# Attention's row maxima handed over by halves of a unit, four places for the split projection parts, and stack loads behind both transfers

## The reference

```
xn = layernorm(x)
xh = xn[:, :, :64];  xs = holt(xn)[:, :, :64]        # a smoothing scan over the tokens
s  = attention block: two multi-head attentions (8 heads of 8 numbers each), one over xh, one over xs,
     softmax(q k^T / sqrt(8)) v, output projections, layernorms, feed-forward
g  = silu(mixture of 32 experts, top 4 of 32 for each token, capacity 640 per expert, and a shared expert)
x  = x + s * g
```

## Time and profile before

| | |
|---|---|
| median of 3 runs | 2137.68 us (2133.76 to 2138.3) |
| profiled execution, its own time | 2140.73 us |
| its span, first to last instruction | 2138.9 us |
| PE busy | 1884.9 us (88%) |
| DVE busy | 1776.4 us (83%) |
| ACT busy | 1444.4 us (68%) |
| POOL busy | 344.0 us (16%) |
| mean granted TensorE clock | 0.936 |
| row maxima, first to last reduction | 139.8 to 1394.0 us |
| exponentials, first to last | 186.6 to 1444.2 us |

### The profile page before, as it was taken

How to read it: one execution, slowest core, us unless ns; L and a number is a source line. 1 busy time by engine, 2 the same in 40 slices (tenths; PEclk the granted TensorE clock), 3 DMA queues, 4 the chain that set the end, 5 groups by cost and what they waited for, 6 DMA issues and landing times.

```text
span 2138.9 us, 33478 instructions
## 1 busy us (share of the span) xinstructions
PE 1884.9 (88%) x11734; PEld 719.9 (34%) x11734; DVE 1776.4 (83%) x2689; ACT 1444.4 (68%) x2807; POOL 344.0 (16%) x516
## 2 busy tenths in 40 slices
PE   7537999999999999999999999988997887599884
PEld 6201222222222222222222222216764444266563
DVE  6689999999999999999999999903347887478778
ACT  5204888888888888888888888883322344567542
POOL 1210000000000222222222222000027652000000
PEclk9656999999999999999999999999998889799896
DMA  3231121120010111111111111016754332321321
GB/s 84 83 116 44 46 71 65 47 84 26 25 35 24 40 46 36 46 42 35 51 38 38 49 37 49 8 32 178 205 162 123 108 112 73 101 71 54 101 76 30
DMA packets 145888, 144.01 MB, mean 67 GB/s; under 512 B 29451, under 2 KB 124687, under 8 KB 145572
## 3 DMA queue, kind: packets, MB, share of 16 engines
q1 hardware_dynamic: 137380, 124.71, 19.2%
q0 software_dynamic: 8352, 17.29, 2.7%
HBM read 81.06 MB, written 60.03 MB: 66 GB/s over the span
## 4 chain that ended last, share of the span: by engine, by line
PE 70%; DVE 14%; ACT 8%; issue 3%; DMA 2%; SPq 2%; POOL 1%; DVEq 0%; ACTq 0%
PE PS L1606 23%; PE PS L1633 18%; PE PS L1588 8%; DVE mxp L758 6%; PE PS L1680 3%; ACT probs L1202 3%; ACT SG L1187 2%; PE PS L1736 2%; PE PS L1836 2%; PE PS L1854 1%; PE PS L1667 1%; PE PS L1745 1%; PE PS L1857 1%; PE PS L1839 1%; DMA xs_d<-SG 1%
## 5 line engine op out<-in xcount | busy, mean ns | idle before, releaser
L758 DVE TENSOR_REDUCE mxp<-PS 128x1 f32<-128x1024 f32 x1024 | 1203.5, 1220 | 43.9 <-PE PS L1588 29.2
L1202 ACT ACTIVATE probs<-PS 128x512 f32<-128x512 f32 x2048 | 1061.7, 604 | 168.1 <-PE PS L1633 164.9
L1633 PE MATMUL PS<-stacks 51*128 51x512 bf16 x2048 | 615.8, 383 | 28.2 <-ACT probs L1202 16.8
L1588 PE MATMUL PS<-stacks 48*128 48x512 bf16 x2048 | 518.9, 393 | 49.1 <-DVE mxp L758 30.4
L1606 PE MATMUL PS<-probs,VH 128*32 128x512 f32 x4096 | 546.7, 606 | 6.8 <-ACT SG L1187 6.1
L1633 PEld LDWEIGHTS PS<-stacks 51*128 51x128 bf16 x2048 | 154.3, 94 | 681.1 <-ACT probs L1202 611.7
L1588 PEld LDWEIGHTS PS<-stacks 48*128 48x128 bf16 x2048 | 109.5, 94 | 217.0 <-DVE mxp L758 178.0
L1472 POOL DMA_INDIRECT xe_d<-xn_s,rows_s x128 | 126.0, 984 | 328.5 <-PE PS L1606 292.6
L1497 POOL DMA_INDIRECT VP<-oe_d,ROWI x128 | 133.4, 1042 | 255.7 <-DMA oe_d<-stacks 194.7
L771 DVE TENSOR_TENSOR stacks<-stacks,PS 128x640 f32<-128x640 f32 x32 | 26.2, 820 | 134.7 <-ACT stacks L1234 134.7
L1606 PEld LDWEIGHTS PS<-probs,VH 128*32 128x32 f32 x4096 | 81.6, 108 | 125.0 <-issue 109.2
(11 more groups left out here) (344 smaller groups left out, 1922.4 us busy)
## 6 DMA issues: line engine op xcount, KB each, us to landing
xe_d<-zt SPq DMA_DIRECT2D x16, 640.0 KB
stacks<-xe_d SPq DMA_DIRECT2D x32, 320.0 KB, 3.3
oe_d<-stacks SPq DMA_DIRECT2D x32, 320.0 KB, 2.4
o_d<-SG SPq DMA_DIRECT2D x256, 32.0 KB, 1.6
ews<-in_ew_dram SPq DMA_DIRECT2D x33, 192.0 KB, 2.3
stacks<-ql_d SPq DMA_DIRECT2D x64, 96.0 KB
stacks<-kl_d SPq DMA_DIRECT2D x64, 96.0 KB
probs<-xs_d SPq DMA_DIRECT2D x18, 256.0 KB, 3.7
```

The source lines that it names most:

```text
L758: v.tensor_reduce(mxp[:, n // 2, n % 2:n % 2 + 1], MXB[n % 2].rearrange("p a c -> p (a c)"), X_AX, ALU.max).then_inc(mx_done, 1)
L1202: act.activation(probs[:, at:at + 512], PS[:, bank_of(u, e), :], ACT.Exp, scale=float(1.0 / np.sqrt(np.float32(DK)))).then_inc(exp_done, 1)
L1588: mm = pe.matmul(MXB[n % 2][:, i, :], QS[w][o:o + MAXROWS, (n // 2) * P:(n // 2 + 1) * P], KS[w][o:o + MAXROWS, key:key + 512], start=True ...
L1633: pe.matmul(PS[:, bank_of(u, e), :], KS[w][o:o + KROWS + 3, kt * P:(kt + 1) * P], QS[w][o:o + KROWS + 3, q0:q0 + 512], start=True, stop=Tr ...
```

## The change

Three edits, which depend on each other.

1. The split parts have four places; the two new ones lie in the stack slots 1 to 3, which are not loaded until all stores have landed. ScalarE's `lead(j)` waits for the stores of block j-4.
2. A unit's maxima are handed over in two halves, each of 8 query tiles (16 chunks, 1024 queries). Each half has its own reduction, GpSimd split, transposition, copy and pair of transfers. The unit's second half is turned after exponential 22 of the unit itself (TURNS = (22, 54)) and waited for at exponential 32; the next unit's first half after 54, as before. AHEAD falls from 10 to -6, so 26 chunks are made before the first exponential, and chunks run 16 fewer in front.
3. On SyncE the order for unit u is: clearing stores (first eight units), the second half's maxima of unit u, the loads for unit u+3 (into the slot of unit u-1), first output half, the first half's maxima of unit u+1, second output half.

```diff
-EXPS, TURN, AHEAD = 64, 54, 10
-SLOTS = EXPS + 1
+EXPS, TURNS, AHEAD = 64, (22, 54), -6
+SLOTS = EXPS + 2
...
         def part(parts, level, w):
-            return parts[level][:, w * 512:(w + 1) * 512]
+            if w < 2:
+                return parts[level][:, w * 512:(w + 1) * 512]
+            return QS[1 + level][:, ((parts is KPARTS) * 2 + w - 2) * 512:((parts is KPARTS) * 2 + w - 1) * 512]
...
-            def load_max(u, w):
-                hold(mt_out, u + 1)
+            def load_max(u, w, half, trip):
+                hold(mt_out, 2 * u + half + 1)
+                hold(m_ld[w], 64 * trip + 32 * half)
                 for o in (0, 64):
-                    sp.dma_start(QS[w][o + KROWS:o + KROWS + 3, :], mT[:, :]).then_inc(m_ld[w], 16)
+                    sp.dma_start(QS[w][o + KROWS:o + KROWS + 3, S // 2 * half:S // 2 * (half + 1)], mT[half][:, :]).then_inc(m_ld[w], 16)
...
+                    load_max(u, w, 1, k)
+                    if not last and w > 0 or w == 0 and not (isinstance(k, int) and k == 0):
+                        load_unit(u + 3, 2 * k + (w + 3) // 2, (w + 1) % 2, (w + 3) % 4)
                     store_half(u, g, w % 2, 0)
                     if not (last and w == 3):
-                        load_max(u + 1, (w + 1) % 4)
+                        load_max(u + 1, (w + 1) % 4, 0, k + (w == 3))
                     store_half(u, g, w % 2, 1)
...
-                    if not last:
-                        load_unit(u + 4, g + 2, w % 2, w)
...
-                v.wait_ge(mx_done, CHUNKS * (uu + 1))
-                after(v, spl_ready, uu)
-                v.tensor_reduce(nmx[:, 0, :], mxp[:, :, :], X_AX, ALU.max, negate=True).then_inc(nmx_ready, 1)
+                    if n % (CHUNKS // 2) == CHUNKS // 2 - 1:
+                        half = n // (CHUNKS // 2)
+                        tiles = slice(TCH // 2 * half, TCH // 2 * (half + 1))
+                        v.wait_ge(mx_done, CHUNKS * uu + n + 1)
+                        after(v, spl_ready, 2 * uu + half - 1)
+                        v.tensor_reduce(nmx[:, 0, tiles], mxp[:, tiles, :], X_AX, ALU.max, negate=True).then_inc(nmx_ready, 1)
...
-                after(act, ql_st, 48 * (j - 1))
-                after(act, kl_st, 48 * (j - 1))
+                after(act, ql_st, 48 * (j - 3))
+                after(act, kl_st, 48 * (j - 3))
...
-                    if e == TURN and not final:
-                        act.wait_ge(m_ld[w], 32 * (trip + 1))
-                        write_rows(u + 1, TURN_BANK[u])
+                    if e == TURNS[0]:
+                        after(act, m_ld[(u - 1) % 4], 64 * ((u - 1) // 4 + 1))
+                        write_rows(u, 1, TURN_BANK[u][0])
+                    if e == TURNS[1] and not final:
+                        act.wait_ge(m_ld[w], 64 * trip + 32)
+                        write_rows(u + 1, 0, TURN_BANK[u][1])
...
-                pe.wait_ge(m_ld[w], 32 * (u // 4 + 1))
                 for e in range(EXPS):
-                    after(pe, exp_done, EXPS * u + e - 2 + (TURN < e <= TURN + 2))
-                    if e == TURN + 3 and not final:
-                        pe.wait_ge(mt_out, u + 2)
+                    if e % (EXPS // 2) == 0:
+                        pe.wait_ge(m_ld[w], 64 * (u // 4) + 32 * (e // (EXPS // 2) + 1))
+                    after(pe, exp_done, EXPS * u + e - 2 + any(t < e <= t + 2 for t in TURNS))
+                    if e == TURNS[0] + 3:
+                        pe.wait_ge(mt_out, 2 * u + 2)
+                    if e == TURNS[1] + 3 and not final:
+                        pe.wait_ge(mt_out, 2 * u + 3)
```

More of the change, by code:

```diff
@@ L436, in _ @@
                     for lv in range(3):
[L437 removed]
+                        sp.dma_start(parts[lv, :, j * 512:(j + 1) * 512], part(src, lv, j % 4)).then_inc(stored, 16)
             hold(ql_st, 48 * NB)
@@ L676, in remainder @@
                 for n, (left, parts) in enumerate(((QREST, QPARTS), (KREST, KPARTS))):
-                    ins = v.scalar_tensor_tensor(left[w], PS[:, 4 + 2 * w + n, :], bcol[:, n:n + 1], part(parts, 0, w), ALU.add, ALU.subtract)
+                    ins = v.scalar_tensor_tensor(left[w], PS[:, 4 + 2 * w + n, :], bcol[:, n:n + 1], part(parts, 0, j % 4), ALU.add, ALU.subtract)
                 ins.then_inc(rest, 1)
@@ L1171, in middle @@
                 for left, parts in ((QREST, QPARTS), (KREST, KPARTS)):
-                    ins = act.activation(part(parts, 1, j % 2), left[j % 2], ACT.Copy)
+                    ins = act.activation(part(parts, 1, j % 4), left[j % 2], ACT.Copy)
                 ins.then_inc(part1, 1)
@@ L1431, in _ @@
                 for left, parts in ((QREST, QPARTS), (KREST, KPARTS)):
-                    ins = pool.tensor_tensor(part(parts, 2, j % 2), left[j % 2], part(parts, 1, j % 2), ALU.subtract)
+                    ins = pool.tensor_tensor(part(parts, 2, j % 4), left[j % 2], part(parts, 1, j % 4), ALU.subtract)
                 ins.then_inc(part2, 1)
@@ L1445, in _, with largest @@
             plink = Chain(pool, pool_chain).link
[L1447 to L1452, removed]
-                pool.tensor_tensor(spl[:, 2, :], nmx[:, 1, :], spl[:, 1, :], ALU.subtract).then_inc(spl_ready, 1)
+            def largest(uu, half):
+                tiles = slice(TCH // 2 * half, TCH // 2 * (half + 1))
+                first, second = nmx[:, 0, tiles], nmx[:, 1, tiles]
+                pool.wait_ge(nmx_ready, 2 * uu + half + 1)
+                after(pool, mt_ready, 2 * uu + half - 1)
+                plink(pool.tensor_copy(spl[:, half, 0, :], first))
+                plink(pool.tensor_tensor(second, first, spl[:, half, 0, :], ALU.subtract))
+                plink(pool.tensor_copy(spl[:, half, 1, :], second))
+                pool.tensor_tensor(spl[:, half, 2, :], second, spl[:, half, 1, :], ALU.subtract).then_inc(spl_ready, 1)
             def values(u):
@@ L1469, in scatter @@
                             pool.wait_ge(pv_done, TCH * (u - 3) + 2 * (KTOP * i + n))
-                        if i == 1 and n == 1:
-                            largest(u - 2)
+                        if n == 1:
+                            largest(u - 3 + i, 1 - i)
                         pool.indirect_dma_start(xe_d, bass.IndirectOffsetOnAxis(rows_s[i][:, n:n + 1], 0), xn_s[i][:, :], None,
                                                 bounds_check=E * CAP - 1, oob_is_err=False).then_inc(sc_st[i], 16)
-            for u in range(UNITS // 2):
+            for u in range(3):
                 values(u)
-                if u >= 2:
-                    largest(u - 2)
+            largest(0, 0)
+            for u in range(3, UNITS // 2):
+                values(u)
+                largest(u - 3, 1)
+                largest(u - 2, 0)
             pool.wait_ge(rows_done, 1)
@@ L1484, in _ @@
                 scatter(u)
-            for uu in range(UNITS - 2, UNITS):
-                largest(uu)
+            for uu in range(UNITS - 3, UNITS):
+                largest(uu, 1)
+                if uu + 1 < UNITS:
+                    largest(uu + 1, 0)
             for i in range(2):
@@ L1634, in _ @@
                               start=True, stop=True).then_inc(sc_ready, 1)
-                    if e == TURN and not final:
+                    if e == TURNS[0]:
                         pe.wait_ge(exp_done, EXPS * u + e - 1)
-                        turn_max(u + 1, TURN_BANK[u])
+                        turn_max(u, 1, TURN_BANK[u][0])
+                    if e == TURNS[1] and not final:
+                        pe.wait_ge(exp_done, EXPS * u + e - 1)
+                        turn_max(u + 1, 0, TURN_BANK[u][1])
                     if chunk < min(CHUNKS * UNITS, CHUNKS * (u + 1) + AHEAD + CHUNKS * (e + 1) // EXPS):
```

38 lines of the change are left out of this document (19 added, 19 removed).

## The result

The changed kernel takes 2111.67 us (median of 4 runs, 2110.06 to 2113.83), the kernel before beside it 2137.99 us: ratio 0.9877, 95% interval 0.9864 to 0.989. That is 26.3 us less where 19.3 were forecast; 2111.67 lies in the range and 6.7 us under the number.

The account below looks back on a forecast made before the run. Front waits, lone maxima, then 2048 exponentials at 0.6 us plus extras bound it, no engine full in the loop. -21.5 - 18.1 + 4.6 + 15.7 = -19.3 us: 2121.4 from the profiled run, 2118.4 from the median; range 2109 to 2130.

Parts of the forecast that it names:

- Four places: Front: ScalarE's waits for stores and VectorE's behind them vanish, maxima start at 118.3; -21.5 us, bounds 17.5 to 22.8.
- Fewer first chunks and the wait for the first transfer: Before the first exponential: 16 chunks fewer, -18.1 us; first scores wait behind the DMA backlog ending at 149.7, +4.6.
- no backlog in the way: Rival, first scores: the small transfer passes or the loads end sooner, 4.6 us less, 2113.8 us; chance 0.16.
- Halves in the loop: Loop: 32 more hand-overs at 0.49 us each, +15.7 us, bounds 10.9 to 28.8.
- 0.15 reduction: Loop: extra time of the four-exponential group with a unit's final reduction, 0.15 of the 0.49 us per hand-over.
- halving dearer: Rival, loop: a unit's second hand-over disturbs more, to 0.8 us a unit; +9.9 us, 2128.3; chance 0.14.
- The second wait for a transfer, and the loads behind both: Loop, exponential 32 and SP's queue: 2.3 us cover at the wait, 4.3 left after the loads; costed at nothing.
- The slower rival: Exponential 0 of each unit: stack loads not through at first half's hand-over; 2157 us if loads take 22; chance 0.06.
- What follows only moves: After attention: the rest of the span only shifts in time, its length unchanged; 0 us in the sum.

Follow-up runs that it names:

- e5: Changed kernel with the 2 MB store issued behind the first maxima's transfer; 2111.44 us, ratio 0.9875 to the kernel before.
- e3: Changed kernel without VectorE's wait for its own second small reduction at each unit's end; 2110.42 us, ratio 0.9873 to the kernel before.
- e7: Changed kernel with the stack loads back behind the second half's stores, for unit u+4 at the end of unit u; 2161.75 us, ratio 1.0119 to the kernel before.
- e1: Kernel before with only the four places for the split parts; 2120.62 us, ratio 0.9909 to the kernel before.
- e0: The kernel before, unedited, run and profiled again; 2137.59 us, ratio 0.9997 to the kernel before.
- e12: The changed kernel once more, unedited, beside e6 and e10 on one chip; 2195.84 us, ratio 0.9874 to the kernel before.
- e6: Changed kernel without VectorE's wait at each unit's end and with the 2 MB store behind the first maxima's transfer; 2192.13 us, ratio 0.9859 to the kernel before.
- e10: As e6, with two fewer chunks ahead of the first exponential (AHEAD = -8); 2191.1 us, ratio 0.9849 to the kernel before.

## Why the prediction was right, and where it was off

*Four places.* Right in kind: all six waits fell, and the ranks' matmuls then set L734. The term was 2.6 us too large: 18.9, not 21.5. The selection ends 3.2 us later than forecast, and L734 follows the ranks' matmuls 0.5 us sooner. Most of the 3.2 us can be added up from VectorE's rows: L718 (three times 1.53 for 0.69), L722 (three times 2.06 for 1.23) and L725 (1.53 for 0.69) are 5.9 us longer, and five of the six of L717 and L721 are 0.57 each shorter, 3.0 in all. Before, it was these that were long, beside GpSimd's remainders:

```profile
65.24 1.16 POOL L1432 TENSOR_TENSOR SG<-wa,HH 128x512 bf16<-128x512 f32 x1 [6.86 <-ACT wa L1172]
65.54 1.21 DVE L716 TENSOR_REDUCE EK<-probs 128x32 bf16<-128x1024 bf16 x1
...
66.78 1.80 DVE L717 TENSOR_TENSOR probs<-iob,EK 128x1024 bf16<-128x1024 bf16 x1
```

So the 5.6 us a block that I took over held one such clash a block, and without the waits other instructions meet the remainders, with a dearer clash. A remainder is longer too, 2.14 us for 1.16; the one that starts 0.1 us behind L717 or L721 is lengthened and they are not. A VectorE reduction with one input, L716 above, keeps its 1.21 beside a remainder. "SBUF — State Buffer" of the Trainium skill ("Who interferes with whom") has this as a rule: a VectorE instruction with two SBUF inputs contends with a GpSimd instruction that reads SBUF. The rows agree for L717 before and for L718 and L722 after; L725 has one tensor input and is outside this rule, and why it takes 1.53 was not tried. That the clashes are the cause is read off the overlap; no run took the remainders away.

*Fewer first chunks and the wait for the first transfer.* -13.2 against -13.5, and e5 and the packets showed the cause that I had named, the loads and behind them the store. That the size fits to 0.3 us is in part luck. The loads came 19.2 us earlier and not 22.8 (by the figures that the prediction gives, 20.2 and 1.2, it should have said 21.4), so the backlog ended 3.5 us after the forecast 149.7; the scores were needed 2.7 us after the forecast 146.3, because the front was late as well. The two errors nearly cancel. The rival "no backlog in the way" is refuted for the changed kernel.

*Halves in the loop.* +9.9 us against +15.7; this is the step that was mis-sized. "0.15 reduction" was read off the one group that held a reduction and also the wait at the unit's end. The rows after separate them, 2.40 against 2.53, and e3 removes 0.12 a unit by removing that wait. What is new is 0.33 for the transposition, and 32 times that is 10.6 us. The rival "halving dearer" has no row for it. The 2.7 us of slack that the prediction gave VectorE in a unit, for its lower bound, is 1.6 by the earlier trace rows ((1177.6 - 1130.0) / 30); the sum didn't use it.

*The second wait for a transfer, and the loads behind both.* Cost nothing in the changed kernel, as forecast: the wait before the first scores is the only one for L470's transfers in its list. The slower rival was the right thing to fear: with the loads ahead of the second half's transfer on the queue (e7) it cost 50 us.

*What follows only moves: not so.* In my sum the rest of the span was constant. It was 694.2 before and 687.3 after, and 685.7 to 693.0 over eight kernels timed at about 2110 to 2160 us whose code there is one and the same. Matching instruction by instruction, 1.4 us of the difference have come up 25 us behind the last weighing and 2.8 more between 165 and 195; at 566 it is still 4.1, and the rest comes up behind that, mostly between 570 and 590. Here the same two places of three kernels, 180 to 189 and 566 to 580 us behind the last weighing (the clock is the column behind GpSimd's). Before:

```profile
1624.70:1633.70 9.00, 7.61 (x18) 3.62 (x16) 6.43 (x33) 3.33 (x6) 6.41 (x7) 0.63 0.56 165
2010.70:2024.70 14.00, 7.41 (x17) 3.63 (x18) 9.41 (x29) 3.74 (x5) 0.00 (x0) 0.62 0.58 188
```

After:

```profile
1602.60:1611.60 9.00, 8.08 (x32) 4.22 (x33) 8.72 (x37) 2.94 (x6) 6.95 (x7) 1.00 0.60 168
1988.60:2002.60 14.00, 12.01 (x43) 6.43 (x42) 13.59 (x46) 8.75 (x12) 0.00 (x0) 0.92 0.71 230
```

e1, the four places alone:

```profile
1606.60:1615.60 9.00, 7.78 (x18) 3.69 (x17) 6.43 (x33) 3.15 (x5) 5.27 (x6) 0.64 0.57 160
1992.60:2006.60 14.00, 8.15 (x17) 3.92 (x18) 9.41 (x29) 3.74 (x5) 0.00 (x0) 0.50 0.58 188
```

Where TensorE has the clock at 1.00 or near it, it does 32 and 43 matmuls in the window; at 0.5 to 0.64 it does 18 and 17. Whether the higher clock makes the work faster there, or earlier work brings the clock up, the rows don't part, and what in the changed kernel shifts it is open. The seven kernels with the halves have 685.7 to 691.3, the three executions without them (before, e0, e1) 692.8 to 694.2, so it goes with the halves, by how much varies, and it isn't shown to be theirs. So of the 26.3 us, about 22 lie within attention, where the edits are, and the rest behind it, which no term of the sum held; without it the forecast would have been some 3 us off and not 6.7.

## What to carry to other kernels

A small transfer that the next step waits for must not be queued behind large ones that run on few DMA engines: place on the queue was worth 50 us here, more than the edits gained together. When a wait is removed, ask what will now run side by side: an engine's own time per block holds the clashes with its neighbours as they fell, and these fall elsewhere afterwards. And when a price is read off a group that holds two unusual things, find another group that holds only one.

## What the runs showed of the hardware that was not expected

The last three kernels of the table ran in one comparison, and in it the kernel before (2225.75 us) took 88 us more than at first and the changed kernel (e12) 84 us more, with the ratio as it was (0.9874 and 0.9877). e6 and e10 have the same long last stretch. e12's expected 2111 to 2113 us were missed for this reason. Attention in e12 ends at 1422.7, as in the changed kernel; all of it lies behind, from 1574 us on. The same two windows in the kernel after, and then in e12:

```profile
1574.00:1584.00 10.00, 8.94 (x44) 5.70 (x42) 5.47 (x9) 3.08 (x4) 7.86 (x8) 1.00 0.95 273
1584.00:1594.00 10.00, 3.71 (x18) 2.68 (x18) 6.98 (x31) 0.21 (x1) 7.56 (x9) 0.70 0.42 116
```

```profile
1574.00:1584.00 10.00, 4.89 (x19) 3.26 (x19) 1.38 (x2) 0.60 (x1) 7.57 (x9) 0.79 0.97 270
1584.00:1594.00 10.00, 2.85 (x4) 0.67 (x2) 0.69 (x1) 0.00 (x0) 7.71 (x8) 0.67 0.21 58
```

TensorE, VectorE and ScalarE stand still for most of the second window while GpSimd issues its gathers at the same rhythm, and the timeline of e12 finds no releaser inside the core:

```profile
1598.88 0.60 ACT L1257 ACTIVATE SG<-PS 128x512 f32<-128x512 f32 x1 [18.34 <-remote]
```

What they waited for was not found. The ratio to the kernel before, taken side by side, was the same all the same.
